# Causal attention: single-bank score tiles, a ring of four PSUM banks, and row maxima of head pairs in 32x32 tiles

## The chip, the cores and the metric

The kernel runs on one core of a Trainium2 chip. The metric is device time in microseconds (us). PE is TensorE, DVE VectorE, ACT ScalarE, POOL GpSimd and SP SyncE. PSUM, where matmuls write, has 8 banks of 512 fp32 columns.

## What is computed

Two "macaron" layers over 2048 tokens of 128 features: a feed-forward part, causal attention, a feed-forward part. The attention of the first layer, cut to what matters (the second differs in bias and in having no output projection):

```python
N_HEADS = 16; HEAD_DIM = D // N_HEADS          # 8
scores = jnp.einsum('bhqd,bhkd->bhqk', q, k)   # t = 2048 queries and keys
scores = jnp.where(causal, scores, -jnp.inf)
attn = jax.nn.softmax(scores / np.sqrt(HEAD_DIM).astype(np.float32), axis=-1)
ctx = jnp.einsum('bhqk,bhkd->bhqd', attn, v)
...
x = x + _L0_attn_ref(_layernorm(x, axis=-1), ...)
x = x + _L1_attn_ref(_layernorm(x, axis=-1), L1_attn_W, L1_attn_b)
```

## The kernel before

The change is in `attention_layer` and in the planner ahead of it. The 16 heads form four groups of four, and the queries four chunks of 512. A *step* is a pair (group g, chunk c). `STEPS` goes through the chunks upward for groups 0 and 1, then downward for groups 2 and 3. Each head holds 32 partitions of `q_slots` and `k_slots`: its 8 dimensions with 4 rows each, all 32 of which a matmul can contract at once.

A step has two kinds of work:

- **Maxima.** Softmax subtracts each query's maximum, so the scores are first computed with queries on the partitions, and DVE reduces them. A *unit* is a block of 128 queries against up to 512 keys in one PSUM bank. Off the diagonal (key chunk before the query chunk) a unit is one head of 512 keys; on the diagonal it is one head of 512 or 384 keys, two of 256 or four of 128, and gets a mask (L1943). A unit is written by matmuls of 128 rows by 32 columns, one per 32 queries (L1937), and reduced by one instruction (L2057). All DVE work that reads PSUM in this stage goes through a *ring* of three banks (5 to 7). `ring_full` counts filled banks, `ring_read` emptied ones; the same ring carries the turned maxima ("max"), the outputs ("out") and in the first layer the projection ("turned", "project").
- **Quads.** A *quad* is four heads, 128 keys and up to 512 queries (on the diagonal 512, 384, 256, 128). Scores now have keys on the partitions: one matmul of 32 rows per head (L1887), with masks on the diagonal (L1902). They are taken two heads at a time: `score_tile(q, 0)` and `score_tile(q, 1)`, each with two banks of banks 0 to 3. ACT takes the exponential of two heads by one instruction (L2019) and counts `exp_done`. `values` (L1916) multiplies the exponentials of the *previous* quad into bank 4.

The units of a step are done two steps ahead (`AHEAD`), strewn over the quads by `units_beside_quads` after a pace of columns. A *turn* is one quad with its units and other ring items; a layer has 160 turns with a quad, the first 36 of which (steps up to group 0, chunk 2) are called the early part below, and the other 124 the late part. PE runs each turn's instructions strictly as written, and so do ACT and DVE:

```python
score_tile(q, 0)
score_tile(q, 1)
...
for item in items[:half]:
    ring_item(item)
if previous:
    values(previous)
for item in items[half:]:
    ring_item(item)
```

Half the items, rounded up, stand ahead of `values`. On a diagonal quad `mask_tile(q, 0)` goes first and `mask_tile(q, 1)` follows the scores. PE's waits in a turn are `exp_done` ahead of scores and values, and `ring_read` ahead of each ring item.

## Time and profile before

| | us |
|---|---|
| median of 3 runs (1183.99 to 1186.95) | 1186.41 |
| the profiled execution | 1190.67 |
| its span in the trace | 1188.8 |
| PE, DVE, ACT busy in the span | 1055.3, 987.5, 657.2 |
| reductions (L2057), 1120 | 675.2 |
| exponentials (L2019), 640 | 539.1 |
| PE: units (L1937), values (L1916), scores (L1887) | 389.2, 290.4, 140.6 |

Busy time is the union of an engine's instructions. On PE it includes the time in which a matmul's last columns run through the array, so that a busy PE can still be waiting. The two attention stages take about 194 to 581 us and 771 to 1154 us of the span.

### The profile page before, as it was taken

The numbers are of one execution on the slowest core, as the hardware profiler recorded it, in microseconds if no ns is written. First come the engines' busy times: TensorE is split into PE (matmuls) and PEld (weight loads), VectorE is DVE, ScalarE is ACT, GpSimd is POOL, SyncE is SP. The second block draws the span as 40 slices with busy tenths as digits, with TensorE's granted clock in tenths as the row PEclk, the third lists the DMA queues.
The fourth block names the chain that finished last, engine by engine and source line by source line (L and its number), as shares of the span: only waits on it lengthen the run. The fifth ranks groups of instructions, "written<-read, shape, count | busy, mean of one in ns | idle before, by whom it ended". The sixth has DMA issues, their size and how long they took to land.

```text
span 1188.8 us, 34469 instructions
## 1 busy us (share of the span) xinstructions
PE 1055.3 (89%) x14718; PEld 484.3 (41%) x14718; DVE 987.5 (83%) x2314; ACT 657.2 (55%) x844; POOL 101.2 (9%) x109
## 2 busy tenths in 40 slices
PE   1999977999999999999798848699999999999987
PEld 1455543333333333334446735333333333333436
DVE  8977478999999999987544766899999999998852
ACT  0322223556787777787423213246677778777773
POOL 6111011000000000000042252000000000000000
PEclk9999998999999999999998978899999999999999
DMA  5430043000000000000001023220000000000001
GB/s 162 160 160 1 1 151 100 3 3 3 2 2 2 3 2 3 2 2 4 1 27 46 28 73 96 64 64 3 2 3 3 3 2 2 3 2 3 3 2 36
DMA packets 29492, 36.67 MB, mean 31 GB/s; under 512 B 3694, under 2 KB 26388, under 8 KB 29084
## 3 DMA queue, kind: packets, MB, share of 16 engines
q1 hardware_dynamic: 27228, 29.22, 7.4%
q0 software_dynamic: 2112, 5.25, 1.6%
q8 instruction: 117, 1.92, 0.7%
q14 instruction: 35, 0.29, 0.1%
HBM read 15.29 MB, written 18.87 MB: 29 GB/s over the span
## 4 chain that ended last, share of the span: by engine, by line
PE 48%; DVE 41%; issue 5%; ACT 3%; DMA 1%; another core or an unknown queue 1%; POOL 0%; SPq 0%; DVEq 0%; ACTq 0%; POOLq 0%
DVE part_max L2057 27%; PE psum L1916 12%; PE psum L1937 11%; PE psum L1887 6%; PE psum L518 3%; PE psum L1902 2%; PE psum L1569 2%; ACT hidden L2019 2%; DVE xn L204 2%; PE psum L1964 1%; PE psum L1168 1%; PE psum L542 1%; DVE norm_v L169 1%; PE psum L1943 1%; PE psum L299 1%
## 5 line engine op out<-in xcount | busy, mean ns | idle before, releaser
L2057 DVE TENSOR_REDUCE part_max<-psum 128x1 f32<-128x512 f32 (+3 forms) x1120 | 675.2, 666 | 38.0 <-PE psum L1943 21.9
L2019 ACT ACTIVATE hidden<-psum 128x1024 f32<-128x1024 f32 (+3 forms) x640 | 539.1, 895 | 220.4 <-PE psum L1887 219.5
L1937 PE MATMUL psum<-k_slots,q_slots 128*32 128x512 f16 (+3 forms) x5120 | 389.2, 353 | 27.7 <-DVE part_max L2057 14.9
L1916 PE MATMUL psum<-hidden,v_aug 128*9 128x512 f32 (+3 forms) x2560 | 290.4, 530 | 0.1
L1937 PEld LDWEIGHTS psum<-k_slots,q_slots 128*32 128x32 f16 x5120 | 123.1, 95 | 284.8 <-DVE part_max L2057 200.6
L1887 PE MATMUL psum<-q_slots,k_slots 32*128 32x512 f16 (+3 forms) x1472 | 140.6, 328 | 9.9 <-ACT hidden L2019 7.9
L1943 PE MATMUL psum<-ident_bf,later_keys 128*32 128x128 bf16 (+2 forms) x1408 | 90.3, 247 | 0.0
L518 PE MATMUL psum<-parts,w_parts 128*128 128x512 f16 x384 | 88.6, 381 | 0.6 <-DVE parts L931 0.6
L1887 PEld LDWEIGHTS psum<-q_slots,k_slots 32*128 32x128 f16 x1472 | 42.1, 91 | 99.2 <-ACT hidden L2019 46.4
L1902 PE MATMUL psum<-later_keys,ident_bf 128*32 128x128 bf16 x2048 | 74.8, 223 | 4.4 <-ACT hidden L2019 1.9
L1916 PEld LDWEIGHTS psum<-hidden,v_aug 128*9 128x9 f32 x2560 | 61.8, 90 | 34.3 <-ACT hidden L2019 1.6
L1902 PEld LDWEIGHTS psum<-later_keys,ident_bf 128*32 128x32 bf16 x2048 | 39.7, 95 | 50.4 <-issue 20.0
L518 PEld LDWEIGHTS psum<-parts,w_parts 128*128 128x128 f16 x384 | 36.4, 98 | 39.9 <-issue 1.4
L662 ACT CAST parts<-psum 128x512 f16<-128x512 f32 x32 | 18.6, 588 | 53.9 <-PE psum L503 53.9
L1943 PEld LDWEIGHTS psum<-ident_bf,later_keys 128*32 128x32 bf16 x1408 | 37.9, 98 | 18.5 <-issue 17.5
L1631 POOL TENSOR_TENSOR x_plus<-x_res,fb_half 128x512 f32<-128x512 f32 x7 | 9.3, 1323 | 389.3 <-DVE xn L204 389.3
L315 ACT COPY xn_t<-psum 128x512 f32<-128x512 f32 x8 | 4.7, 586 | 65.2 <-PE psum L290 65.2
L1611 ACT ACTIVATE hidden<-psum,bias_cols 128x512 f32<-128x512 f32 x32 | 20.0, 688 | 32.8 <-PE psum L1559 32.8
L1234 ACT ACTIVATE hidden<-psum,unscale 128x512 f32<-128x512 f32 x24 | 16.1, 686 | 35.9 <-PE psum L1156 26.5
L1569 PE MATMUL psum<-tw_t,hidden 128*128 128x128 f32 x256 | 30.4, 278 | 3.4 <-ACT hidden L1611 3.4
L1569 PEld LDWEIGHTS psum<-tw_t,hidden 128*128 128x128 f32 x256 | 29.6, 194 | 5.1 <-issue 2.9
L1559 PE MATMUL psum<-parts,tw_t 128*128 128x512 f16 x64 | 18.3, 438 | 12.1 <-DVE parts L1536 10.5
(277 smaller groups left out, 866.1 us busy)
## 6 DMA issues: line engine op xcount, KB each, us to landing
expert_regions<-k_slots SPq DMA_DIRECT2D x2, 4096.0 KB, 17.9
q_slots<-q_rows SPq DMA_DIRECT2D x8, 512.0 KB, 3.9
k_slots<-k_rows POOLq DMA_DIRECT2D x28, 128.0 KB, 4.1
q_slots<-in_L_ffn_W_dram SPq DMA_DIRECT2D x2, 1024.0 KB, 6.7
q_rows<-parts SPq DMA_DIRECT2D x6, 256.0 KB, 2.6
k_rows<-parts SPq DMA_DIRECT2D x6, 256.0 KB, 2.8
q_slots<-expert_regions SPq DMA_DIRECT2D x20, 64.0 KB, 1.8
sorted_rows<-xn SPq DMA_DIRECT2D x5, 256.0 KB, 2.3
```

Of the source, the lines that this page charges most:

```text
L204: return dve.tensor_scalar(dst[:, b, :], src[:, b, :], s.mean_var[:, b, 0:1], s.rstd[:, b:b + 1], ALU.subtract, ALU.mult)
L518: last = pe.matmul(psum[:, t, :], w1_parts[:, e, wp, t * P:(t + 1) * P], x_mask[:, k % NX, xp, :], start=(e == 0 and (wp, xp) == (0, 0)), ...
L662: act.copy(mask_sb[:, k % NX, :], psum[:, MASK_BANKS + k % 2, :]).then_inc(mask_ready, 1)
L1569: last = pe.matmul(down_bank(n)[:, i * D:(i + 1) * D], hidden[:, n % 2, t, i * P:(i + 1) * P], tw2_t[:, t, :], start=(t == 0), stop=(t == ...
L1611: act.activation(hidden[:, n % 2, t, :], psum[:, t, :], ACT.Relu, bias=fb1_col[:, t:t + 1], scale=1.0 / X_SCALE).then_inc(relu_done, 1)
L1887: last = pe.matmul(psum[:, S_BANKS + 2 * (tile % 2) + par, cols], k_slots[rows, G * g + 2 * pr + par, j * P:(j + 1) * P], q_slots[rows, g, ...
L1902: last = pe.matmul(psum[rows32(m), S_BANKS + 2 * (tile % 2) + par, off:off + P], ident_bf[:, rows32(m)], later_keys[:, :], start=(pr == 0) ...
L1916: last = pe.matmul(psum[VW * h:VW * h + DH + 1, O_BANK, off:CH], v_aug[:, j, G * g + h, :], probs[:, (2 * n + h // 2) % NP, h % 2, off:CH] ...
L1937: last = pe.matmul(psum[rows32(m), bank, a * w:(a + 1) * w], q_slots[:, g, qb * P + m * SLOT:qb * P + (m + 1) * SLOT], k_slots[:, G * g + ...
L1943: last = pe.matmul(diagonal_part(psum[rows32(m), bank, 0:heads * w], heads), later_keys[:, rows32(m)], repeated(ident_bf, heads), start=Fa ...
L2019: act.activation(probs[:, tile % NP, :, off:CH], psum[:, bank:bank + 2, off:CH], ACT.Exp, scale=scale).then_inc(exp_done, 1)
L2057: dve.tensor_reduce(part_max[:, step_no[s] % 2, h0:h0 + heads, i, kc], psum[:, bank, 0:heads * w].rearrange("p (a k) -> p a k", a=heads), ...
```

## The change

Score tiles become one bank each, three in number (banks 0 to 2, `S_TILES`), one head per tile. ACT takes the exponential of one head per instruction, and each head's scores wait for the exponential of the head three before it. Bank 3 is now the output's (`O_BANK`), and the ring has banks 4 to 7.

Off-diagonal units become *pairs*: two heads, each contracted over its own 32 rows, so that eight matmuls of 32 rows by 32 columns write two neighbouring banks, and one reduction reads both (2 x 512 columns). A pair takes two ring slots, beginning at an even one; a diagonal unit still takes one. Within a turn, pairs stand ahead of diagonal units. The plan prices a pair as two units, so the pace is about the same.

In PE's order, the first half of the ring items moves between `score_tile(q, 0)` and `score_tile(q, 1)`. Further, the last chunk's v projection uses bank 0 (bank 3 before), the clearing of the output bank moves to a later place on DVE, and PE waits for the first three chunks' v to be read before the turns begin.

```diff
-                    heads = CH // unit_width(step, i, kc)
+                    heads = CH // unit_width(step, i, kc) if kc == step[1] else 2
...
+        def banks_of_unit(u):
+
+            return 2 if u[2] < u[0][1] else 1
...
-            S_BANKS, O_BANK, RING_BANKS, RING = 0, 4, 5, 3
+            S_TILES, O_BANK, RING_BANKS, RING = 3, 3, 4, 4
...
-                RING_ITEMS.append([("scores", u) for u in units] + [("max", s) for s in turn_max] +
-                                  [("out", s) for s in turn_out])
+                RING_ITEMS.append([("scores", u) for u in sorted(units, key=banks_of_unit, reverse=True)] +
+                                  [("max", s) for s in turn_max] + [("out", s) for s in turn_out])
...
-                    ring_no[item] = len(ring_no)
+                    ring_no[item] = ring_slots[0]
+                    ring_slots[0] += banks_of_item(item) + (ring_slots[0] % 2 if banks_of_item(item) == 2 else 0)
+                    ring_end[item] = ring_slots[0]
...
-                    tile = 2 * n + pr
-                    if tile >= 2:
-                        pe.wait_ge(exp_done, tile - 1)
...
                         for par in range(2):
+                            tile = G * quad_no[q] + 2 * pr + par
+                            if cols.start == off and not masked and tile >= S_TILES:
+                                pe.wait_ge(exp_done, tile - S_TILES + 1)
                             rows = rows_of(2 * pr + par)
-                            last = pe.matmul(psum[:, S_BANKS + 2 * (tile % 2) + par, cols],
+                            last = pe.matmul(psum[:, tile % S_TILES, cols],
...
-                    pe.wait_ge(exp_done, 2 * n + 2)
+                    pe.wait_ge(exp_done, G * (n + 1))
...
-                    if n >= RING:
-                        pe.wait_ge(ring_read, n - RING + 1)
+                    if ring_end[item] > RING:
+                        pe.wait_ge(ring_read, ring_end[item] - RING)
...
+                        for m, a in itertools.product(range(COLS), range(heads) if both else ()):
+                            rows = rows_of(h0 + a)
+                            last = pe.matmul(psum[rows32(m), both, :][:, a, :],
+                                             q_slots[rows, g, qb * P + m * SLOT:qb * P + (m + 1) * SLOT],
+                                             k_slots[rows, G * g + h0 + a, kc * CH:(kc + 1) * CH], start=True, stop=True)
...
                         score_tile(q, 0)
+                    for item in items[:half]:
+                        ring_item(item)
+                    if q:
                         score_tile(q, 1)
                     if q in diagonal:
                         mask_tile(q, 1)
-                    for item in items[:half]:
-                        ring_item(item)
...
-                            bank = S_BANKS + 2 * (tile % 2)
-                            act.activation(probs[:, tile % NP, :, off:CH], psum[:, bank:bank + 2, off:CH],
+                            act.activation(probs[:, (2 * n + h // 2) % NP, h % 2, off:CH], psum[:, tile % S_TILES, off:CH],
                                            ACT.Exp, scale=scale).then_inc(exp_done, 1)
...
+                        if kind == "scores" and banks_of_item(item) == 2:
+                            s, i, kc, h0, heads = what
+                            dve.tensor_reduce(part_max[:, step_no[s] % 2, h0:h0 + heads, i, kc], psum[:, pair_banks(item), :],
+                                              axis=AX.X, op=ALU.max).then_inc(ring_read, slots_of_item(item))
```

On PE, a full-width turn with four off-diagonal units stood like this before (L1887 scores, L1937 units, L1916 values), with the next turn's scores as its last row:

```order
L1887 MATMUL psum<-q_slots,k_slots 128x512 x4
L1937 MATMUL psum<-k_slots,q_slots 32x512 x8
L1916 MATMUL psum<-hidden,v_aug 9x512 x4
L1937 MATMUL psum<-k_slots,q_slots 32x512 x8
L1887 MATMUL psum<-q_slots,k_slots 128x512 x4
```

Now the same kind of turn stands like this (L1907 scores, L1957 pairs, L1936 values; the bracket names the semaphore that a row waits for):

```order
L1907 MATMUL psum<-q_slots,k_slots 128x512 [waits exp_done_90] x2
L1957 MATMUL psum<-k_slots,q_slots 32x512 [waits ring_read_85]
L1957 MATMUL psum<-k_slots,q_slots 32x512 x7
L1907 MATMUL psum<-q_slots,k_slots 128x512 [waits exp_done_90] x2
L1936 MATMUL psum<-hidden,v_aug 9x512 [waits exp_done_90]
L1936 MATMUL psum<-hidden,v_aug 9x512 x3
L1957 MATMUL psum<-k_slots,q_slots 32x512 [waits ring_read_85]
L1957 MATMUL psum<-k_slots,q_slots 32x512 x7
L1907 MATMUL psum<-q_slots,k_slots 128x512 [waits exp_done_90] x2
```

The four score matmuls, adjacent before, now come two and two with a pair between them. The last one of a quad, its fourth head, waits for the exponential of the same quad's first head, since three tiles serve four heads.

A narrow diagonal turn (128 queries) had its two groups of masks (L1902) around four score matmuls, with the unit behind them:

```order
L1902 MATMUL psum<-later_keys,ident_bf 32x128 x8
L1887 MATMUL psum<-q_slots,k_slots 128x128 x4
L1902 MATMUL psum<-later_keys,ident_bf 32x128 x8
L1937 MATMUL psum<-k_slots,q_slots 32x512 x4
L1916 MATMUL psum<-hidden,v_aug 9x256 x4
```

Now the unit (L1962, with its mask L1968) stands between the score matmuls (L1907), and masks are L1922:

```order
L1922 MATMUL psum<-later_keys,ident_bf 32x128 x8
L1907 MATMUL psum<-q_slots,k_slots 128x128 x2
L1962 MATMUL psum<-k_slots,q_slots 32x512 x4
L1968 MATMUL psum<-ident_bf,later_keys 32x128 x4
L1907 MATMUL psum<-q_slots,k_slots 128x128 x2
L1922 MATMUL psum<-later_keys,ident_bf 32x128 x8
L1936 MATMUL psum<-hidden,v_aug 9x256 x4
```

Here too the scores are split by the ring item, and the second mask and the values come behind the second half.

## Rows read from the trace of the kernel before

**Rows 1.** The page: span, and the granted TensorE clock in 40 slices (tenths).
```profile
span 1188.8 us, 34469 instructions
...
PEclk9999998999999999999998978899999999999999
```

**Rows 2.** Windows, early and late part of both attention layers: busy time per engine.
```profile
194.50:297.40 102.90, 96.19 (x1732) 36.37 (x1728) 101.50 (x185) 58.82 (x76) 2.17 (x4) 1.00 0.07 21
297.40:581.00 283.60, 275.33 (x4452) 105.65 (x4448) 255.19 (x499) 216.08 (x259) 2.51 (x2) 0.99 0.01 3
771.30:874.20 102.90, 96.20 (x1732) 36.43 (x1728) 101.42 (x185) 58.81 (x76) 2.17 (x4) 1.00 0.07 21
874.20:1153.80 279.60, 270.29 (x4420) 101.52 (x4424) 252.00 (x495) 216.46 (x259) 3.15 (x3) 1.00 0.01 3
```

**Rows 3.** Chain of waits, shares by line: first layer, early part, then late part.
```profile
by line: DVE part_max L2057 85.2%; issue 3.8%; PE psum L1937 3.1%; PE psum L1916 2.5%; PE psum L1964 1.1%; DVE nm_parts L2078 0.8%; PE psum L1887 0.7%; PE psum L1902 0.7%; DVE xn L2090 0.6%; DVE nm_parts L2076 0.6%; DVE neg_max L2101 0.5%; 
...
by line: PE psum L1916 24.9%; DVE part_max L2057 23.6%; PE psum L1937 20.9%; PE psum L1887 11.4%; PE psum L1902 4.3%; ACT hidden L2019 3.8%; issue 2.6%; PE psum L1964 2.3%; PE psum L1943 2.3%; PE psum L1958 1.1%; PE psum L1953 0.6%; PE psum
```

**Rows 4.** Groups by line and shape: busy us, mean ns | idle before, releasers.
```profile
L2057 DVE TENSOR_REDUCE part_max<-psum 128x1 f32<-128x512 f32 x896 | 554.9, 681 | 21.9 <-PE psum L1937 10.4 <-PE psum L1943 7.5
L2019 ACT ACTIVATE hidden<-psum 128x1024 f32<-128x1024 f32 x448 | 434.5, 1024 | 140.1 <-PE psum L1887 139.7
...
L2057 DVE TENSOR_REDUCE part_max<-psum 128x1 f32<-128x384 f32 x128 | 65.1, 549 | 10.0 <-PE psum L1943 9.3
...
L2019 ACT ACTIVATE hidden<-psum 128x512 f32<-128x512 f32 x64 | 34.7, 595 | 37.0 <-PE psum L1887 37.0
```

**Rows 5.** Timeline, DVE: four reductions back to back (start, us, engine).
```profile
429.98 2.47 DVE L2057 TENSOR_REDUCE part_max<-psum 128x1 f32<-128x512 f32 x4
```

**Rows 6.** Timeline, ACT: two instructions of 512 columns back to back.
```profile
501.23 1.09 ACT L2019 ACTIVATE hidden<-psum 128x512 f32<-128x512 f32 x2 [0.64 <-PE psum L1887]
```

**Rows 7.** Timeline, a full-width turn of four units, from its scores to the next.
```profile
341.20 0.42 PE L1887 MATMUL psum<-q_slots,k_slots 32*128 32x512 f16 x4
...
341.63 1.94 ACT L2019 ACTIVATE hidden<-psum 128x1024 f32<-128x1024 f32 x2 [0.45 <-PE psum L1887]
...
343.60 0.42 PE L1887 MATMUL psum<-q_slots,k_slots 32*128 32x512 f16 x4
```

**Rows 8.** Chain of waits in order of time, late part: start, us, what.
```profile
508.35 0.59 PE psum L1964 x4
...
510.22 1.03 ACT hidden L2019
511.25 0.05 issue
511.29 0.39 PE psum L1887 x2
...
512.34 0.86 PE psum L1916 x8
513.20 0.22 PE psum L1937 x4
513.41 0.06 PE psum L1943 x4
513.47 0.33 PE psum L1887 x4
```

**Rows 9.** Timeline, PE: masks and scores of a diagonal quad (384 queries wide).
```profile
561.35 0.28 PE L1902 MATMUL psum<-later_keys,ident_bf 128*32 128x128 bf16 x8
561.57 0.29 PE L1887 MATMUL psum<-q_slots,k_slots 32*128 32x128 f16 x6
561.79 0.29 PE L1902 MATMUL psum<-later_keys,ident_bf 128*32 128x128 bf16 x8
```

**Rows 10.** Windows of the exponentials' line alone, the two late parts: ACT busy (x).
```profile
297.40:581.00 283.60, 212.23 (x248) 0.99 0.01 3
...
874.20:1153.80 279.60, 212.61 (x248) 1.00 0.01 3
```

More of the change, by code:

```diff
@@ L272, in t_bank, with v_bank @@
                 return psum[:, self.beside if n == 0 else 0, :]
+            def v_bank(self, n):
+                return psum[:, 0 if n == NCH - 1 else 3, :]
             def qk_bank(self, n, m):
@@ L307, in values @@
                     b = n * BPC + i
-                    last = pe.matmul(psum[:, self.V_BANK, i * D:(i + 1) * D], xn_t[:, b * P:(b + 1) * P],
+                    last = pe.matmul(self.v_bank(n)[:, i * D:(i + 1) * D], xn_t[:, b * P:(b + 1) * P],
                                      self.w_qkv[:, 2, :], start=True, stop=True)
@@ L1934, in ring_item @@
                         qb = BPC * c + i
-                        for a in range(heads):
+                        both = pair_banks(item) if kc < c else None
+                        for m, a in itertools.product(range(COLS), range(heads) if both else ()):
[3 more added lines that the diff above has]
+                                             k_slots[rows, G * g + h0 + a, kc * CH:(kc + 1) * CH], start=True, stop=True)
+                        for a in range(0 if both else heads):
                             for m in range(COLS):
@@ L1950, in ring_item @@
                     elif kind == "turned":
-                        pe.wait_ge(ring_read, ring_no["out", (NG - 1, what)] + 1)
+                        pe.wait_ge(ring_read, ring_end["out", (NG - 1, what)])
                         for i in range(BPC):
@@ L1954, in ring_item @@
                     elif kind == "project":
-                        pe.wait_ge(ring_read, ring_no["turned", what] + 1)
+                        pe.wait_ge(ring_read, ring_end["turned", what])
                         for i in range(BPC):
@@ L2012, in _ @@
                         off = first_query(q)
[L2013 to L2014 removed]
+                        for h in range(G):
+                            tile = G * n + h
                             act.wait_ge(scores_done, tile + 1)
[L2016 to L2019 removed]
+                            if n >= NP // 2 and h == 0:
+                                act.wait_ge(pv_done, n - NP // 2 + 1)
+                            act.activation(probs[:, (2 * n + h // 2) % NP, h % 2, off:CH], psum[:, tile % S_TILES, off:CH],
                                            ACT.Exp, scale=scale).then_inc(exp_done, 1)
```

71 lines of the change are left out of this document (37 added, 34 removed).

## The prediction

> **What bounds the kernel now.** The page gives a span of 1188.8 us and a granted clock that falls only outside the two attention stages [rows 1]. The change touches these alone, so I cut them, with the busy-time windows, into the early part of each layer (36 turns) and the late part (124 turns). PE runs there at a granted clock of 0.99 to 1.00, its level of 2.4 GHz. Early, DVE is busy 101.5 of 102.9 us: nothing else can set the time. Late, it is busy 255.2 of 283.6 and 252.0 of 279.6 us, while PE shows 275.3 and 270.3 [rows 2]. The chain of waits agrees: early, 85.2% of it is the reduction L2057; late, that falls to 23.6%, and PE's values, units and scores (24.9, 20.9 and 11.4%) lead [rows 3]. So the early 2 x 103 us are worth what DVE is worth, and the late 2 x 282 us what PE's order of work is worth, with its waits. The exponentials' line has 248 instructions in each late part, two to a turn [rows 10]: a late turn lasts 283.6 / 124 = 2.29 us and 279.6 / 124 = 2.25 us.
>
> **Part 1: one reduction for a pair.** Four reductions of 512 columns take 2.47 us [rows 5] and one takes 0.681 [rows 4], so they follow each other every (2.47 - 0.68) / 3 = 0.597 us. From 384 to 512 columns a reduction grows from 0.549 to 0.681 us [rows 4], 1.03 ns a column; 1024 columns should take 0.597 + 0.53 = 1.13 us. A pair thus saves 2 x 0.597 - 1.13 = 0.065 us of DVE. No row shows a reduction over two banks; ACT's rows do show two banks read at no loss (0.595 us for 512 columns, 1.024 for 1024 [rows 4], 0.84 ns a column). I take 0.065, with 0 as the other end. Off-diagonal units are 768 in the program (16 c for each step of chunk c, four groups, two layers), so 384 pairs: 25 us of DVE if all of it counted. By the planned order 63 pairs of a layer stand in the early part, where it counts: 63 x 0.065 = 4.1 us a layer. PE's own chain there, made as below, comes to 96 of the 103 us, near enough to take some back. I book -3 a layer.
>
> The Trainium skill (VectorE: DVE Perf Modes, the section on the TRN2 errata) gives a VectorE instruction that reads PSUM 120 cycles ahead of its columns, 125 ns at 0.96 GHz. By that a pair would save 0.125 us and the early part 8 us a layer, and the forecast would be 8 us lower. The rows show half of it, because instructions back to back overlap part of their fixed time; the sum goes by the rows.
>
> **Part 2: pairs in 32x32 tiles.** A unit of four column tiles costs PE 0.22 us on the chain [rows 8], the stream of 512 columns once: the four run side by side. No row shows eight tiles of 32x32. Bounds: 0.22 us a pair if all eight run side by side, as four row tiles already do in the scores (0.42 us for four, one stream and its run-out [rows 7]), or 0.44 if they go as four and four. I take 0.22, since both dimensions are shown apart.
>
> **Part 3: scores cut in two, three tiles for four heads.** This is the term that decides. The fourth head's scores need the tile that the first head of the same quad holds, so inside every turn PE must see the first head's scores go to ACT and come back. Rows give each leg. From the start of the scores to ACT's start: 341.20 to 341.63, 0.43 us [rows 7]. One exponential of 512 columns: 0.595 us [rows 4]. From its end to PE: 0.05 us, after which the released scores, the values (0.86 us) and a unit (0.22) follow one another on the chain [rows 8]. The round trip is 0.43 + 0.60 + 0.05 = 1.08 us. Before, PE issued four heads at once and had a whole turn until it needed them again.
>
> What lies in those 1.08 us is the first half of the ring items, one pair in most turns: scores 0.33 (0.22 and 0.11 until a matmul of another tile shape starts [rows 8]), pair 0.22 + 0.11. That is 0.66; two items make 0.88 to 0.99. PE stands for the rest. Then come the last scores, 0.33, the values, 0.86, and the second half. A full turn with a pair on either side, against four units before:
>
> 1.08 + 0.33 + 0.86 + (0.11 + 0.22 + 0.11) = 2.71 us, where 341.20 to 343.60 shows 2.40 [rows 7].
>
> DVE would need 2 x 1.13 = 2.26 us for such a turn, so it would idle and PE's chain set the pace.
>
> Over the late part, by the planned order of a layer's 80 full turns: about 28 have one pair behind the values (0.44), 29 one diagonal unit (0.22 + 0.06 + 0.11 = 0.39 [rows 8]), 5 nothing, and 18 transposes or two items (0.59 us for four transposes [rows 8]; 0.5 to 1.1, taken as 0.75). The mean is (12.3 + 11.3 + 13.5) / 80 = 0.46, and a full turn 2.27 + 0.46 = 2.73 us. The 44 diagonal turns scale with their width w: masks 0.22 [rows 9], latency 0.22 + 0.21 w, exponential 0.595, 0.49, 0.38 or 0.27 (by 0.84 ns a column), 0.05, scores 0.21 w + 0.11, masks 0.11, values 0.86 w, and 0.23 behind: 2.83, 2.38, 1.97 and 1.53 us, mean 2.18. Sum: 80 x 2.73 + 44 x 2.18 = 314 us, against 283.6. The second layer has no projection, some 4 us less: 310 against 279.6. That is +31 a layer.
>
> The price that no row shows is the change of tile shape around pairs. Bounds: 0, or the 0.11 us seen from 32x128 to 128x32. With 0, the 40 pairs behind values in a late part lose 0.22 each, 9 us a layer. I take 0.11. The Trainium skill (TensorEngine Tiling (Array Packing), Key Properties) says that changing the tiling mode drains TensorE; by that the 0.11 holds for 32x32 as well, and speaks against this change, which goes from two such changes a turn to about five.
>
> **Part 4: ACT.** Two instructions of 512 columns back to back take 1.09 us [rows 6], 0.50 apart, so four need about 2.0 us a full turn. That hides in 2.7 us.
>
> **Part 5: the rest.** The later clearing of the output bank is the same DVE instruction in another place. The wait for v puts PE behind three copies that DVE must do ahead of its first reduction anyway. Cost 0 to 1 us a layer; I take 0. A fourth ring bank holds 2.26 us of DVE work instead of 1.8: that helps an early part that is already full, so nothing.
>
> **Sum.** 2 x (31 - 3) = +56 us on the profiled execution's own 1190.67 (1.9 of it outside the span): 1246.7. The median of the runs is 4.3 lower, so 1242.
>
> **Rivals.**
> - *Faster: the round trip is covered.* If PE has 1.08 us of work or ring waits between the halves, the late part follows PE's bare sum: 1.08 gives way to some 0.79, and the mean turn of 314 / 124 = 2.53 us to 2.24, where 2.27 is the mean before. That is 248 turns x 0.03 = -7 us late and -6 early, and up to -12 more where the ring's fourth bank also takes waits from DVE's share of the late chain: 1161 to 1173. For it: the order puts items exactly there, and where two stand (some 30 of 80) they nearly cover it. Against: one pair leaves 0.4 us uncovered. It decides at a round trip of about 0.84 us.
> - *No change.* Those gains and part of the stall cancel: 1183 to 1190. It needs the tile change at 0 everywhere and half the stall covered, and the rows show 0.11.
> - *Pairs go as four and four.* 40 late pairs behind the values, 0.22 each, make +9 a layer; early PE's chain becomes 96 + 63 x 0.22 = 110, over DVE's 103, so +7 instead of -3 there: 1242 + 2 x (9 + 10) = 1280. For it: no row of such tiles. Against: rows and columns each overlap.
> - *Tile changes at 0 around pairs.* 1242 - 18 = 1224, still slower.
>
> **How the numbers follow.** Stall as summed, 1215 to 1272: 0.62 (tile changes at 0 included). Four and four, 1270 to 1290: 0.09. A smaller loss, 1190 to 1215: 0.08. No change: 0.06. Faster: 0.15. A measurement of this kernel can tell 0.3%, 3.6 us, from no change. So faster 0.15, same 0.06, slower 0.79. The range 1183 to 1280 leaves out the faster case and half of four and four.
>
> **What would show it.** Right: in the late parts the PE rows of the scores (L1907) wait for the exponentials (L2045) in nearly every turn, at 0.2 to 0.4 us; the late turns average 2.5 us; DVE falls from 90% busy there to about (255 - 8) / 314 = 79%; a pair's reduction (L2082) lasts 0.681 + 0.53 = 1.21 us. Wrong: late turns at 2.2 us with the scores' waits gone, pairs' matmuls starting 0.43 us apart (four and four), or early parts that grow.

## The result, and the profile after

| us | before | after |
|---|---|---|
| median, 4 runs each | 1185.58 (1183.99 to 1186.95) | 1399.01 (1390.11 to 1404.01) |
| profiled execution, its span | 1190.67, 1188.8 | 1390.11, 1388.4 |
| mean granted clock, whole span | 0.973 | 0.904 |
| early part, mean of the two layers | 103.1 | 134.6 |
| late part, mean of the two layers | 281.4 | 348.8 |

The parts are cut here at the first exponential of a part's first turn, which moves the bounds of [rows 2] by up to 0.4 us. The changed kernel is slower by a ratio of 1.179, 95% interval 1.172 to 1.186. The prediction, 1242 us with a range of 1183 to 1280, had the sign and missed the size by 157 us. Of e3 and e12 below, one run of two lies over 1.5% above the other and is the one that was profiled: the faster run is the one compared, and their parts are left out. A first sign stands on the page of the changed kernel: the granted clock falls inside both attention stages (about slices 6 to 20 and 25 to 39), where it had been all but full [rows 1].

```profile
span 1388.4 us, 34747 instructions
...
PEclk9999879868899999999789978897999589899998
```

The windows of the four parts, with the columns of [rows 2] (window, its length, then busy time and instructions of PE, PEld, DVE, ACT and POOL, then the granted clock, DMA share, GB/s):

```profile
200.00:335.60 135.60, 115.72 (x1764) 38.90 (x1757) 105.62 (x129) 66.80 (x149) 2.18 (x4) 0.82 0.06 16
335.60:680.10 344.50, 324.43 (x4414) 106.57 (x4414) 248.81 (x363) 239.12 (x507) 2.50 (x2) 0.96 0.01 2
865.90:999.50 133.60, 113.25 (x1772) 39.35 (x1760) 105.71 (x130) 66.59 (x148) 2.18 (x4) 0.86 0.05 16
999.50:1352.50 353.00, 333.22 (x4380) 102.95 (x4378) 245.22 (x358) 239.93 (x507) 3.82 (x3) 0.91 0.01 2
```

Both parts of both layers grow: early +32.7 and +30.7, late +60.9 and +73.4 us, together 198 of the 200 us between the two profiled executions. DVE is no longer full in the early part (105.6 of 135.6 us; before 101.5 of 102.9). The mean clock of 0.82 to 0.96 lies between TensorE's two levels. With full as 2.4 GHz and half as 1.2, a mean c over a window of length w means 2 (1 - c) w at half: 49 + 28 + 37 + 64, some 178 us (the trace's clock records, less rounded, give 181).

The chain of waits by line, early and late part of the first layer, answers to [rows 3]: early, the reductions (L2082 and L2087) fall from 85.2% to 32.7%, and PE's values, pairs, scores and units (L1936, L1957, L1907, L1962) take their place.

```profile
by line: DVE part_max L2082 25.5%; PE psum L1936 18.5%; PE psum L1957 12.5%; PE psum L1907 11.2%; PE psum L1962 7.4%; issue 7.4%; DVE part_max L2087 7.2%; PE psum L1922 3.8%; PE psum L1968 3.1%; PE psum L1989 1.2%; DVE xn L2120 0.4%; DVE nm
```
```profile
by line: PE psum L1936 28.2%; PE psum L1907 24.6%; PE psum L1957 10.0%; DVE part_max L2082 10.0%; PE psum L1962 7.7%; PE psum L1922 4.2%; issue 3.7%; PE psum L1968 2.5%; PE psum L1989 2.3%; ACT hidden L2045 2.0%; DVE part_max L2087 1.8%; PE
```

The groups by shape, beside [rows 4]: a pair's reduction lasts 1.222 us, and one-bank exponentials 0.601 us. ACT's idle time ahead of the exponentials, mostly for scores, is 237.5 us in this shape alone.

```profile
L2045 ACT ACTIVATE hidden<-psum 128x512 f32<-128x512 f32 x896 | 475.3, 601 | 237.5 <-PE psum L1907 222.8 <-PE psum L1922 13.2
L2082 DVE TENSOR_REDUCE part_max<-psum 128x2 f32<-128x1024 f32 x384 | 458.8, 1222 | 103.3 <-PE psum L1957 96.8 <-issue 0.6 <-PE psum L1968 0.4
...
L1957 PE MATMUL psum<-k_slots,q_slots 32*32 32x512 f16 x3072 | 165.5, 413 | 44.0 <-DVE part_max L2082 38.7 <-DVE part_max L2087 2.9 <-DVE nm_parts L2108 0.2
...
L2087 DVE TENSOR_REDUCE part_max<-psum 128x1 f32<-128x512 f32 x128 | 84.9, 686 | 38.8 <-PE psum L1968 37.9
```

The timeline of a few turns of the early part (start, length, engine, line) shows how both engines come to stand. A diagonal unit (L1962, read by L2087) has taken one ring slot, so the pair behind it skips one. That pair is written at 241.64. The next pair, at 243.59, has waited 1.54 us for DVE's L2082, and the only L2082 that ends there (242.32 + 1.22 = 243.54) is the reduction of the pair just before it. While PE waits, ACT gets no scores (1.74 us idle), and then DVE has nothing to read (0.60 us idle): the waits of three engines follow one another.

```profile
240.72 0.40 PE L1962 MATMUL psum<-k_slots,q_slots 128*32 128x512 f16 x4
...
241.10 0.39 PE L1907 MATMUL psum<-q_slots,k_slots 32*128 32x512 f16 x2
241.50 0.68 DVE L2087 TENSOR_REDUCE part_max<-psum 128x1 f32<-128x512 f32 x1
...
241.64 0.41 PE L1957 MATMUL psum<-k_slots,q_slots 32*32 32x512 f16 x8 [0.15 <-DVE part_max L2082]
...
242.32 1.22 DVE L2082 TENSOR_REDUCE part_max<-psum 128x2 f32<-128x1024 f32 x1
...
243.59 0.41 PE L1957 MATMUL psum<-k_slots,q_slots 32*32 32x512 f16 x8 [1.54 <-DVE part_max L2082]
...
243.93 0.39 PE L1907 MATMUL psum<-q_slots,k_slots 32*128 32x512 f16 x2
244.14 1.23 DVE L2082 TENSOR_REDUCE part_max<-psum 128x2 f32<-128x1024 f32 x1 [0.60 <-PE psum L1957]
...
244.35 1.08 ACT L2045 ACTIVATE hidden<-psum 128x512 f32<-128x512 f32 x2 [1.74 <-PE psum L1907]
```

### The profile page after: what moved, and what is told of

Same layout as the page of the kernel before. It is cut to its first block, busy times and chain, and to the rows that moved or that the text cites. A ratio compares the mean times of both kernels' runs of the same rounds, so it can differ in the third digit from the quotient of the medians.

```text
span 1388.4 us, 34747 instructions
## 1 busy us (share of the span) xinstructions
PE 1212.8 (87%) x14718; PEld 499.2 (36%) x14718; DVE 983.5 (71%) x1930; ACT 719.7 (52%) x1484; POOL 101.8 (7%) x109
## 4 chain that ended last, share of the span: by engine, by line
PE 65%; DVE 23%; issue 6%; ACT 2%; POOL 1%; DMA 1%; SPq 1%; DVEq 0%; ACTq 0%; POOLq 0%
PE psum L1936 18%; PE psum L1907 15%; DVE part_max L2082 10%; PE psum L1957 7%; PE psum L1962 6%; DVE part_max L2087 3%; PE psum L1922 3%; PE psum L520 3%; PE psum L1968 2%; PE psum L1571 2%; PE psum L1989 2%; DVE xn L205 1%; PE psum L544 1%; PE psum L1561 1%; PE psum L1170 1%
## 5 line engine op out<-in xcount | busy, mean ns | idle before, releaser
L2045 ACT ACTIVATE hidden<-psum 128x512 f32<-128x512 f32 (+3 forms) x1280 | 602.0, 535 | 356.1 <-PE psum L1907 293.3
L2082 DVE TENSOR_REDUCE part_max<-psum 128x2 f32<-128x1024 f32 x384 | 458.8, 1222 | 103.3 <-PE psum L1957 96.8
L1936 PE MATMUL psum<-hidden,v_aug 128*9 128x512 f32 (+3 forms) x2560 | 321.8, 579 | 0.1
L1907 PE MATMUL psum<-q_slots,k_slots 32*128 32x512 f16 (+3 forms) x1472 | 299.0, 347 | 8.6 <-ACT hidden L2045 6.0
L2087 DVE TENSOR_REDUCE part_max<-psum 128x1 f32<-128x384 f32 (+3 forms) x352 | 215.7, 638 | 107.5 <-PE psum L1968 105.3
L1957 PE MATMUL psum<-k_slots,q_slots 32*32 32x512 f16 x3072 | 165.5, 413 | 44.0 <-DVE part_max L2082 38.7
L1962 PE MATMUL psum<-k_slots,q_slots 128*32 128x128 f16 (+3 forms) x2048 | 139.6, 331 | 33.4 <-DVE part_max L2082 22.1
L1907 PEld LDWEIGHTS psum<-q_slots,k_slots 32*128 32x128 f16 x1472 | 80.9, 92 | 193.4 <-ACT hidden L2045 88.0
L1957 PEld LDWEIGHTS psum<-k_slots,q_slots 32*32 32x32 f16 x3072 | 42.8, 89 | 197.9 <-DVE part_max L2082 118.3
L1962 PEld LDWEIGHTS psum<-k_slots,q_slots 128*32 128x32 f16 x2048 | 51.6, 102 | 141.0 <-DVE part_max L2082 50.2
L1968 PE MATMUL psum<-ident_bf,later_keys 128*32 128x128 bf16 (+2 forms) x1408 | 97.5, 265 | 0.0
L1922 PE MATMUL psum<-later_keys,ident_bf 128*32 128x128 bf16 x2048 | 78.4, 230 | 4.0 <-ACT hidden L2045 1.5
L1936 PEld LDWEIGHTS psum<-hidden,v_aug 128*9 128x9 f32 x2560 | 43.9, 91 | 49.9 <-issue 39.6
L1922 PEld LDWEIGHTS psum<-later_keys,ident_bf 128*32 128x32 bf16 x2048 | 38.4, 97 | 56.1 <-issue 22.7
L1968 PEld LDWEIGHTS psum<-ident_bf,later_keys 128*32 128x32 bf16 x1408 | 40.8, 103 | 26.5 <-issue 25.2
L1236 ACT ACTIVATE hidden<-psum,unscale 128x512 f32<-128x512 f32 x24 | 16.2, 687 | 36.5 <-PE psum L1158 27.0
```

Of the source, the lines that this page charges most:

```text
L1907: last = pe.matmul(psum[:, tile % S_TILES, cols], k_slots[rows, G * g + 2 * pr + par, j * P:(j + 1) * P], q_slots[rows, g, c * CH + cols.s ...
L1922: last = pe.matmul(psum[rows32(m), tile % S_TILES, off:off + P], ident_bf[:, rows32(m)], later_keys[:, :], start=(pr == 0), stop=(pr == 1))
L1936: last = pe.matmul(psum[VW * h:VW * h + DH + 1, O_BANK, off:CH], v_aug[:, j, G * g + h, :], probs[:, (2 * n + h // 2) % NP, h % 2, off:CH] ...
L1957: last = pe.matmul(psum[rows32(m), both, :][:, a, :], q_slots[rows, g, qb * P + m * SLOT:qb * P + (m + 1) * SLOT], k_slots[rows, G * g + h ...
L1962: last = pe.matmul(psum[rows32(m), bank, a * w:(a + 1) * w], q_slots[:, g, qb * P + m * SLOT:qb * P + (m + 1) * SLOT], k_slots[:, G * g + ...
L1968: last = pe.matmul(diagonal_part(psum[rows32(m), bank, 0:heads * w], heads), later_keys[:, rows32(m)], repeated(ident_bf, heads), start=Fa ...
```

## The experiments

All fourteen runs, in the order in which they are told; "over before" is the difference to the runs of before made beside them on the same chip. Parts are means of the two layers, cut as above; the time at the half clock is that of the four parts, from the clock records.

| kernel | median us (range) | over before | early | late | half clock |
|---|---|---|---|---|---|
| changed kernel | 1399.0 (1390.1 to 1404.0) | 213 | 134.6 | 348.8 | 181 |
| e1: pairs over 128 rows | 1362.1 (1361.3 to 1363.0) | 175 | 129.3 | 339.7 | 33 |
| e2: before, units over 32 rows | 1226.3 (1224.5 to 1228.2) | 40 | 108.2 | 297.0 | 55 |
| e3: changed, values first | 1436.9 (of 1436.9, 1460.4) | 250 | | | |
| e4: e1, values first | 1398.1 (1395.6 to 1400.5) | 211 | 129.9 | 357.9 | 39 |
| e5: four one-bank tiles | 1195.1 (1193.8 to 1196.5) | 9 | 103.3 | 284.3 | 3 |
| e6: e5, scores split | 1268.8 (1265.5 to 1272.1) | 83 | 112.5 | 312.3 | 14 |
| e7: three tiles, single maxima | 1289.4 (1283.4 to 1295.3) | 104 | 104.1 | 330.5 | 21 |
| e8: e1, scores adjacent | 1532.7 (1531.5 to 1533.8) | 347 | 155.1 | 398.6 | 123 |
| e9: e1, skipped slot given back | 1319.4 (1318.8 to 1319.9) | 135 | 115.7 | 332.6 | 7 |
| e10: e1, pair read in two | 1331.4 (1327.3 to 1335.4) | 147 | 119.6 | 333.9 | 31 |
| e11: e1, pairs by head | 1300.6 (1296.9 to 1304.2) | 116 | 109.4 | 329.4 | 7 |
| e12: changed, skipped slot given back | 1331.5 (of 1331.5, 1354.9) | 147 | | | |
| e13: e12 again | 1339.2 (1329.1 to 1343.9) | 153 | 116.6 | 344.4 | 120 |
| e14: e11 over 32 rows | 1331.5 (1331.1 to 1340.0) | 145 | 114.7 | 340.1 | 92 |

**Stalls or tiles?** The first theory (T1) takes the prediction's round trip as what sets the pace, and adds that the clock falls because PE stalls. The rival (T2): the tiles of 32 rows bring the clock down themselves. The edit of e1, which also makes a pair two streams of 512 columns on PE where it was one, and that of e2 in the kernel before:

```diff
-                        for m, a in itertools.product(range(COLS), range(heads) if both else ()):
+                        for a, m in itertools.product(range(heads) if both else (), range(COLS)):
...
-                                             q_slots[rows, g, qb * P + m * SLOT:qb * P + (m + 1) * SLOT],
-                                             k_slots[rows, G * g + h0 + a, kc * CH:(kc + 1) * CH], start=True, stop=True)
+                                             q_slots[:, g, qb * P + m * SLOT:qb * P + (m + 1) * SLOT],
+                                             k_slots[:, G * g + h0 + a, kc * CH:(kc + 1) * CH], start=True, stop=True)
```
```diff
+                            rows = rows_of(h0) if kc < c else slice(0, P)
...
-                                                 q_slots[:, g, qb * P + m * SLOT:qb * P + (m + 1) * SLOT],
-                                                 k_slots[:, G * g + h0 + a, kc * CH:kc * CH + w],
+                                                 q_slots[rows, g, qb * P + m * SLOT:qb * P + (m + 1) * SLOT],
+                                                 k_slots[rows, G * g + h0 + a, kc * CH:kc * CH + w],
```

> The changed kernel with one part undone: a pair's eight matmuls contract all 128 rows (tiles of 128x32, four and then four), as units did before; pairs, ring, score tiles and order stay. Theory T1 (the round trip to ACT in every turn sets the pace, and PE's halved clock follows from its stalls): a pair costs PE 0.22 us more, mostly inside the stall; clock still falls to half in the attention stages, time 1390 to 1430. Rival T2 (32x32 tiles themselves make the clock fall): granted clock full through both stages as before, time 1290 to 1340.

> The kernel before with one part of the change done: off-diagonal units contract the 32 rows of their own head (tiles of 32x32, four at a time), all else as before. T1: time within 6 us of before and the clock full in the stages, since DVE still sets the early part and nothing new is waited for. T2: the granted clock falls to half in parts of both stages and the time rises above 1220.

Both theories missed e1's size. Without 32x32 tiles most of the clock is back (33 us at half) and 37 us with it, though a pair now costs PE more; but 175 us of loss stay: they lie in how the work is arranged. In e2 the order is that of before, and the tiles of 32 rows alone cost 40 us and bring the clock down. So the edit to 32-row tiles does lower the clock, as T2 says, for a small part of the time.

e3 and e4 put the values ahead of the second half of the scores, to fill the round trip:

```diff
+                    if previous:
+                        values(previous)
                     if q:
                         score_tile(q, 1)
                     if q in diagonal:
                         mask_tile(q, 1)
-                    if previous:
-                        values(previous)
```

> The changed kernel with the previous quad's values put ahead of the second half of the scores, so that 0.86 us more of PE work lie in the round trip. T1: the stall goes, a late turn with two pairs takes about 2.4 us, the clock recovers, time 1180 to 1260. T2: the clock still falls, time 1300 to 1380.

> Both edits: values ahead of the second half of the scores, and pairs by tiles of 128x32. T1: 1190 to 1270, about the time of the run with values first alone, 0 to 40 us above it for the 0.22 us a pair. T2: clear gain over the run with values first alone, full clock, 1190 to 1260.

T1 and T2 both hoped for a gain, and both runs lie above every range: 38 and 36 us slower than with the old order. In e4 the scores' weight loads wait 232.1 us for exponentials, in e1 93.9. The reading, not tested further: the later the second half is issued, the later ACT ends the quad, and the next quad's scores need those tiles.

**Which part of the arrangement?** e5 is the changed kernel with four score tiles, a ring of three and single maxima over 128 rows, in the order of before, which leaves of the change ACT's finer instructions and the small moves (v's bank and wait, the clearing): all three pieces of the diff below. e6 has the first two, and so splits the scores again; e7 the second alone (three tiles, a ring of four, single maxima); e8 is e1 with the third.

```diff
-            S_TILES, O_BANK, RING_BANKS, RING = 3, 3, 4, 4
+            S_TILES, O_BANK, RING_BANKS, RING = 4, 4, 5, 3
...
-                    heads = CH // unit_width(step, i, kc) if kc == step[1] else 2
+                    heads = CH // unit_width(step, i, kc)
...
                         score_tile(q, 0)
+                        score_tile(q, 1)
...
                     for item in items[:half]:
                         ring_item(item)
-                    if q:
-                        score_tile(q, 1)
```

> The changed kernel with four one-bank score tiles, maxima one head at a time over 128 rows in a ring of three, and both halves of the scores ahead of the ring items: of the change only the one-bank exponentials are left (4 x 0.535 instead of 2 x 1.09 us). A (three banks for four heads cost the time), B (pairs cost it) and C (ring items between the halves cost it) all expect the time of before within 10 us, 1180 to 1197 us, and a clock near 0.97. If it is over 1210 us, the finer exponentials and the waits on them are themselves a part of the loss, and all three lack it.

> The kernel with four one-bank tiles and single maxima, but half of a turn's ring items stand between the two halves of its scores, as in the changed kernel. C: PE's waits for VectorE in the ring now hold back the second half of the scores and starve ScalarE, so the two waits add: at least 1230 us, with the early part over 112 us a layer. A and B: with a bank for each head nothing waits longer, within 12 us of the kernel with four tiles and adjacent halves.

> The changed kernel with maxima one head at a time (128 rows, one bank, ring of four banks) in place of pairs; three score banks and the split order stay. B: without pairs most of the structural loss is gone; what stays is the round trip, under 1250 us, the early part near 105 us a layer. A and C: the three banks or the split order carry it, so it stays over 1300 us with the early part over 120 us, about 20 us under the changed kernel with 128-row pairs (1362 us) at the most for the finer grain of the ring.

> The changed kernel with 128-row pairs and both halves of the scores adjacent, ahead of the ring items. The second half's last head now waits for the first head's exponential with nothing in between, so PE pays the round trip (some 0.6 to 1.1 us) in each of 160 turns a layer. C: the added waits of the split go, and the early part, where VectorE sets the pace, falls from 129 to under 112 us; the late part stays at 340 us or rises by up to 30. A: both parts rise, over 1400 us in all. B: within 25 us of 1362 us, early part still over 122 us.

e5 is near before, as all expected. e6 has C's numbers: splitting the scores costs 74 us though every head has a bank. PE's rows of one late turn show the price of it. In e5 four scores are followed 0.43 us later by the next matmul (421.60 to 422.03; 0.11 of it is the fourth head's wait for an exponential), the last mask is followed by the values 0.05 us later (422.51 to 422.56), and the turn lasts 2.36 us, to 423.96:

```profile
421.60 0.50 PE L1907 MATMUL psum<-q_slots,k_slots 32*128 32x512 f16 x4
422.03 0.35 PE L1962 MATMUL psum<-k_slots,q_slots 128*32 128x384 f16 x4
...
422.51 0.23 PE L1968 MATMUL psum<-ident_bf,later_keys 128*32 128x128 bf16 x4
422.56 1.03 PE L1936 MATMUL psum<-hidden,v_aug 128*9 128x512 f32 x8
...
423.96 0.56 PE L1907 MATMUL psum<-q_slots,k_slots 32*128 32x512 f16 x4
```

In the same turn of e6 each half of two takes 0.32 us (443.29 to 443.61, 444.26 to 444.58), 0.64 in all, the same mask is followed by scores, 0.16 us later (444.10 to 444.26), and the turn lasts 2.70 us, to 445.99:

```profile
443.29 0.39 PE L1907 MATMUL psum<-q_slots,k_slots 32*128 32x512 f16 x2
443.61 0.34 PE L1962 MATMUL psum<-k_slots,q_slots 128*32 128x384 f16 x4
...
444.10 0.23 PE L1968 MATMUL psum<-ident_bf,later_keys 128*32 128x128 bf16 x4
444.26 0.39 PE L1907 MATMUL psum<-q_slots,k_slots 32*128 32x512 f16 x2
444.58 1.05 PE L1936 MATMUL psum<-hidden,v_aug 128*9 128x512 f32 x8
...
445.99 0.39 PE L1907 MATMUL psum<-q_slots,k_slots 32*128 32x512 f16 x2
```

Four row tiles share one stream of columns; two and two need two. That is 0.21 us of the 0.34 by which this turn grew, and the one more change of tile shape, 0.16 against 0.05, is another 0.11. Added up over all turns of the two traces, the time from a group of scores to the next other matmul grows by 48 of the 74 us, that at ring items by 26. e7 then goes against C and A in the early part: it is split and has three banks, yet that part takes 104.1 us, 8 less than e6's with a ring of three. Its late part takes 18 more (330.5 against 312.3). So the 25 us that the early part of e1 has over e7 belong to the pairs, as B said, while B's 1250 us for e7 left out the split. e8 comes out as A alone expected, both parts longer and over 1400 us: with nothing between the halves, PE pays the round trip in full (196.6 us of idle time straight ahead of the scores, 320 waits in 320 turns), ACT waits 455.3 us for scores, and DVE 258.7 for pairs.

**What of the pairs?** The timeline shown for the changed kernel suggested S: the skipped slot counts as read only with the pair behind it, so the next pair finds its slots free only when that pair has been read. By the planned order a layer has 13 skips early and 25 late. e9 gives the slot back with the item before it; e10 has a pair read by two instructions, the first of which gives back the skip and the first bank; e11 fills, counts and reads each head by itself at the pair's place.

```diff
-                for item in RING_ITEMS[-1]:
-                    ring_no[item] = ring_slots[0]
-                    ring_slots[0] += banks_of_item(item) + (ring_slots[0] % 2 if banks_of_item(item) == 2 else 0)
-                    ring_end[item] = ring_slots[0]
+            for item, follows in zip(in_order, in_order[1:] + [None]):
+                ring_no[item] = ring_slots[0]
+                ring_slots[0] += banks_of_item(item)
+                if follows and banks_of_item(follows) == 2:
+                    ring_slots[0] += ring_slots[0] % 2
+                ring_end[item] = ring_slots[0]
...
-                    if ring_end[item] > RING:
-                        pe.wait_ge(ring_read, ring_end[item] - RING)
+                    if ring_no[item] + banks_of_item(item) > RING:
+                        pe.wait_ge(ring_read, ring_no[item] + banks_of_item(item) - RING)
```
```diff
-                            dve.tensor_reduce(part_max[:, step_no[s] % 2, h0:h0 + heads, i, kc], psum[:, pair_banks(item), :],
-                                              axis=AX.X, op=ALU.max).then_inc(ring_read, slots_of_item(item))
+                            for a in range(2):
+                                dve.tensor_reduce(part_max[:, step_no[s] % 2, h0 + a:h0 + a + 1, i, kc],
+                                                  psum[:, bank - 1 + a:bank + a, :], axis=AX.X,
+                                                  op=ALU.max).then_inc(ring_read, 1 if a else slots_of_item(item) - 1)
```
```diff
-                RING_ITEMS.append([("scores", u) for u in sorted(units, key=banks_of_unit, reverse=True)] +
+                RING_ITEMS.append([("scores", u[:3] + (h, 1) if banks_of_unit(u) == 2 else u)
+                                   for u in sorted(units, key=banks_of_unit, reverse=True)
+                                   for h in range(u[3], u[3] + banks_of_unit(u))] +
```

> The changed kernel with 128-row pairs. A pair must begin at an even slot; where it follows an odd number of single units, the slot that it skips now counts as read with the unit before it, and no longer with the pair itself. S (the next pair waits for this very pair's reduction, so the ring holds one pair at each skip: 13 skips in the early part of a layer, 25 in the late part, each some 0.7 to 2 us on VectorE): the early part falls from 129 to 105 to 115 us a layer, in all 1310 to 1335 us, against 1362 without the edit. G (handing over two banks at a time is the cost, skips or not): early part over 122 us, 1350 to 1365 us.

> The changed kernel with 128-row pairs, but VectorE reads a pair with two one-bank reductions, and gives each bank back by itself; the filling, the skips and the placement stay. D (the one instruction over both banks is the cost): under 1310 us, early part under 112 us. S and G: TensorE still waits for both banks and for the skipped slot, so 1350 to 1380 us, the early part within 5 us of 129.

> The changed kernel with every pair filled, handed over and read as two single heads in one bank each (128 rows), at the places in the turns where the pairs stood; no slot is skipped. S and G: near the kernel with three tiles and single maxima, 1280 to 1305 us, early part 103 to 108 us. P (the places of the pairs in the turns cost it): over 1330 us, early part over 118 us.

> The changed kernel as it is, in 32x32 tiles, with the skipped slot counted as read with the unit before it. S: the same gain as with 128-row pairs, 25 to 50 us, 1349 to 1374 us, and less time at the half clock if idle stretches of TensorE bring it; if the 32-row tiles alone bring it, the time at the half clock stays near the 181 us of the changed kernel's attention parts. G: within 12 us of 1399 us.

S holds, with an early part of 115.7 us at the upper end of its range. e9 gives back 43 us, 13.6 of them in each early part, 1.05 us a skip. PE's idle time straight ahead of pairs falls from 36.5 us in e1 to 10.0. Not all of the 43 us need be the wait itself: e1 also spends 26 us more at the half clock than e9, and no run separates the two (at e14's rate below, 31 us for 85, an estimate of 9 us). The same place of the program as in the changed kernel's timeline, in e9: the pair of 234.92 is followed by the next at 235.69, which has waited 0.15 us for the single reduction L2089, and DVE reads two pairs without a gap (x2, 2.35 us, one row).

```profile
234.41 0.39 PE L1910 MATMUL psum<-q_slots,k_slots 32*128 32x512 f16 x2
...
234.92 0.62 PE L1959 MATMUL psum<-k_slots,q_slots 128*32 128x512 f16 x8
234.95 0.69 DVE L2089 TENSOR_REDUCE part_max<-psum 128x1 f32<-128x512 f32 x1
...
235.69 0.61 PE L1959 MATMUL psum<-k_slots,q_slots 128*32 128x512 f16 x8 [0.15 <-DVE part_max L2089]
235.78 2.35 DVE L2084 TENSOR_REDUCE part_max<-psum 128x2 f32<-128x1024 f32 x2
...
236.24 0.39 PE L1910 MATMUL psum<-q_slots,k_slots 32*128 32x512 f16 x2
```

e10 lies outside all expectations, 31 us under e1, and the skip explains at least part of it: the first of its two reductions gives the skipped slot back after about 0.68 us, not 1.22. At the place of the two timelines the next pair waits 1.40 us in e1, 0.87 in e10 and 0.15 in e9. How much of the 31 us that makes over all skips, no run takes apart. e11 shows what a whole pair costs beyond the skip, 19 us. DVE's idle time ahead of these reductions is 76.6 us in e9 and 45.5 in e11, which fits a DVE that waits for both heads; that PE's wait for both banks is the rest is argued. P's 1330 us did not come, but in the early part e11 has 5.3 us more than e7. The windows count 192 DVE instructions there (e11) against 186 (e7): the plan puts more maxima early.

**The clock again.** e12's faster run lies 68 us under the changed kernel, below S's range; e13 repeats it with four runs. e14 is e11 with each head's own 32 rows, as e2 was to before.

> The changed kernel, 32x32 pairs, with the skipped slot counted as read with the unit before it, measured over more rounds. S: 1330 to 1360 us, 40 to 70 us under the changed kernel. If stalls at the skips had brought the half clock, its time in the attention parts falls from 181 us to under 60; if the 32-row tiles bring it by themselves, it stays over 100 us and the kernel stays 15 to 35 us over the one with 128-row pairs and the same skips (1319 us).

> The changed kernel with every pair filled, handed over and read as two single heads, each contracting only its own head's 32 rows in four 32x32 tiles; nothing is skipped and nothing waits for a whole pair. If the 32-row tiles lower the clock by themselves: 1320 to 1350 us against 1301 us with 128 rows, with over 60 us at the half clock. If they do so only where TensorE also stalls for pairs: 1290 to 1310 us, under 30 us at the half clock.

e13 gains 60 us on the changed kernel, stays 20 us over e9, and keeps 120 of the 181 us at the half clock. The rest went when the skipped slot was given back, so stalls, as T1 says, have a part in the clock too. e14 has no pairs and no skips, and its edit to e11 is only in the rows that are contracted: 31 us more, with 92 us at the half clock instead of 7. The windows of e14, and below them those of e11 (the last columns are clock, DMA share, GB/s):

```profile
195.70:310.60 114.90, 112.14 (x1768) 39.70 (x1768) 106.71 (x192) 66.39 (x149) 2.17 (x4) 0.93 0.06 19
310.60:650.80 340.20, 333.18 (x4414) 109.18 (x4410) 255.86 (x492) 237.63 (x507) 2.51 (x2) 0.96 0.01 2
839.10:953.60 114.50, 111.16 (x1768) 39.64 (x1765) 106.82 (x192) 66.40 (x149) 2.17 (x4) 0.94 0.06 19
953.60:1293.50 339.90, 331.92 (x4378) 106.55 (x4374) 252.06 (x488) 237.53 (x507) 3.81 (x3) 0.95 0.01 2
```
```profile
195.70:305.10 109.40, 106.53 (x1768) 41.28 (x1767) 106.55 (x192) 66.69 (x148) 2.18 (x4) 1.00 0.07 20
305.10:634.60 329.50, 324.35 (x4414) 114.18 (x4414) 254.81 (x492) 237.83 (x507) 2.50 (x2) 1.00 0.01 2
820.70:930.10 109.40, 106.53 (x1768) 41.27 (x1770) 106.55 (x192) 66.69 (x148) 2.18 (x4) 1.00 0.07 20
930.10:1259.30 329.20, 323.16 (x4378) 111.34 (x4378) 251.39 (x488) 237.72 (x507) 3.82 (x3) 0.99 0.01 2
```

So the 32-row tiles lower the clock without pairs and skips. The edit does two things, though: in e14 and e2 the units of two heads, on different rows, start 13 ns apart where nothing is waited for, in e11 and before 215 ns apart. PE has less to stream, and its units' weight loads wait longer for DVE (196 against 116 us in e14 and e11, 250 against 201 in e2 and before). Whether the rows or these gaps lower the clock, no run separates.

## Why the prediction was wrong

The step that failed is Part 1, with Part 5's fourth bank at nothing: an early part forecast to gain 3 us a layer lost 31.5, because the skipped slots starved DVE and because the split, the whole pairs and the clock had no early price. In the late part Part 3 had the mechanism and too small a sum, and the clock was missing. Of the 157 us, some 69 lie in the early parts and 73 in the late ones; most of the rest is that the median lies 9 us above the profiled execution after and 4 below it before.

The runs make a ladder from before to after; the third rung changes several things at once. The last two columns are the parts in us a layer. By the differences to before on the same chip, the third rung is 33, the fifth 40 and the last 38:

| rung | kernels | us | early | late |
|---|---|---|---|---|
| one-bank exponentials | before, e5 | +9 | +0.2 | +2.9 |
| scores split | e5, e6 | +74 | +9.2 | +28.0 |
| three tiles, ring of four, places of the pairs | e6, e11 | +32 | -3.1 | +17.1 |
| pairs as wholes, one reduction | e11, e9 | +19 | +6.3 | +3.2 |
| skipped slot given back late | e9, e1 | +43 | +13.6 | +7.1 |
| 32-row tiles, half clock | e1, after | +37 | +5.3 | +9.1 |

A rung's size holds in the company of the rungs under it: with the ring of three in e6 the split costs the early part 9 us that e7's ring of four does not show.

- **Part 3, the round trip: mechanism right, size too small.** The leg between the halves is as summed: in a late turn at full clock the halves start at 407.46 and 408.48, 1.02 us apart (1.08 predicted), and the values follow 0.37 us later. In this turn the pair itself had waited 0.28 us for DVE, so the round trip adds little here.

```profile
407.46 0.39 PE L1907 MATMUL psum<-q_slots,k_slots 32*128 32x512 f16 x2
407.88 1.61 ACT L2045 ACTIVATE hidden<-psum 128x512 f32<-128x512 f32 x3 [0.42 <-PE psum L1907]
...
408.13 0.41 PE L1957 MATMUL psum<-k_slots,q_slots 32*32 32x512 f16 x8 [0.28 <-DVE part_max L2082]
...
408.48 0.45 PE L1907 MATMUL psum<-q_slots,k_slots 32*128 32x512 f16 x2
...
408.85 0.62 PE L1936 MATMUL psum<-hidden,v_aug 128*9 128x512 f32 x4
```

The sign foretold does not stand on PE's score rows: they wait for exponentials 14 times, 6.0 us, since a row counts its run-out as busy. Their weight loads do, 291 times, 88.0 us, but also 241 times, 76.4 us, in e6, where each head has a bank. What tells is when the fourth head starts: in 123 of the 160 full late turns it follows the end of the first head's exponential by under 0.1 us, and is then 0.31 us behind the third head, inside the 0.2 to 0.4 foretold; in e6 it does so in 12. From e6 to e11 the time at the scores grows by 51 us and that at ring items shrinks by 23. But +31 a layer was the whole late price of split and tiles, and these two rungs measured +45: the split alone took 28.
- **"Faster: the round trip is covered", the rival, failed on its bare sum.** e6 has a bank for each head, so there is no such round trip to cover, and its late turns average 312.3 / 124 = 2.52 us, where the bare sum had 2.24 and before 2.27. The second stream of columns for two halves was in the sum of a turn (0.33 twice), but I never weighed it against the single 0.33 of four adjacent scores.
- **Part 1, the early part: the step that failed outright.** I booked -3 and it measured +31.5: 9.2 from the split (3.1 of which the third rung takes back), 6.3 from whole pairs, 13.6 from the skips, 5.3 from the 32-row tiles. The reduction itself was right: 1.222 us a pair, against 1.21. From e11 to e9 DVE's busy time falls by 2.0 (early) and 6.4 us (late) in the first layer's windows, 8.4 / 192 = 0.044 us a pair, somewhat under the 0.065 taken. By the Trainium skill's fixed cost (VectorE: DVE Perf Modes, the TRN2 errata) an estimate of it is 0.125; the trace shows a third of that. What failed is that DVE stays fed. Part 5 counted the ring's fourth bank as 2.26 us of DVE work, two pairs, and so put the ring at nothing; I read in the diff that a pair begins at an even slot, but not what happens to the slot it skips. At a skip the ring holds one pair, and DVE stands still while the next is written.
- **Part 2 and the tile changes: right.** Eight 32x32 tiles are followed by the scores 0.34 us later (243.59 to 243.93 in the changed kernel's timeline above), 0.22 + 0.11 as taken. That refutes "four and four" and "tile changes at 0".
- **The clock: a missing rival.** I carried the 2.4 GHz of [rows 2] into a kernel with other tiles. That is 37 us from e1 to the changed kernel, net of what the 32x32 tiles save PE on a pair.
- **Part 4: nearly right.** e5 costs 9 us where I booked nothing.
- **The signs named.** Late turns average 344.5 / 124 = 2.78 and 2.85 us, not 2.5, and DVE is busy 72 and 69% there, not 79%. "Early parts that grow" was named as a sign of error, and they grew by 31.5 us.

Left open: what the three tiles, the ring of four and the places of the pairs cost each by itself, and how much of the skips' rung is the clock's. No version here beats the kernel before. The pairs' saving on DVE is real (0.044 us each), but with a ring of four and the output's bank three of the eight banks are left, not four, for score tiles.

## What to carry to other kernels

When a ring takes items of two sizes, follow for each skipped slot who gives it back and when: one slot credited to the wrong item cost more here (43 us) than the larger instruction could ever save (384 x 0.044 = 17 us). Matmuls that share a stream because they stand next to each other lose it when other work is put between them, so price an order by PE's time as well as by its waits. An engine that is full before a change is a promise only as long as its buffers stay as deep as the other engines' longest wait.

## What the runs showed of the hardware

With tiles of 32 rows TensorE's clock spent far longer at its lower level than with 128 rows, in the same order of instructions: 92 against 7 us at half (e14, e11), 55 against 3 (e2, before). In the changed kernel, four matmuls of the values (512 columns each) took 1.07 us where the windows give a granted clock of 0.50, and 0.60 at 1.00 (timeline rows, then the windows):

```profile
284.43 1.07 PE L1936 MATMUL psum<-hidden,v_aug 128*9 128x512 f32 x4
```
```profile
247.81 0.60 PE L1936 MATMUL psum<-hidden,v_aug 128*9 128x512 f32 x4
```
```profile
284.40:285.40 1.00, 1.00 (x8) 0.00 (x0) 0.00 (x0) 0.21 (x1) 0.00 (x0) 0.50 0.00 0
247.80:248.40 0.60, 0.60 (x16) 0.11 (x9) 0.60 (x2) 0.42 (x1) 0.00 (x0) 1.00 0.03 7
```

In e14, 85 us more at the half clock came with 31 us more of time. The Trainium skill (TensorE: Matmul & The Clock Gate, A second HAM failure mode: psum-queue depth-cycling) describes a clock that swings because TensorE stands still for moments between groups of matmuls. The trace agrees in e8, whose pairs have 128 rows and whose PE waits most for exponentials (123 us at half). In e2 and e14 the weight loads wait longer for DVE than in before and e11, so the same may be at work there; no run here shows whether fewer rows do it otherwise.
